# Another order for SyncE's placement of the value pieces of batch 0: nine, nine and seven behind the turns and loads of three passes, in place of rows of 8 and 17

## What is computed

```python
x = x + xattn(layernorm(x), ctx_768, Wq, bq, Wk, bk, Wv, bv, Wo, bo)
x = x + ffn(layernorm(x), expert_embeddings, first_linear, second_linear)

# xattn: 16 heads of width 32
attn = softmax(clip(einsum('bhqd,bhkd->bhqk', q, k) * scale))
x = einsum('bhqk,bhkd->bqhd', attn, v).reshape(B, Nq, Cq) @ Wo + bo
```

## Time and profile before

| | us |
|---|---|
| median of three runs | 1437.44 |
| lowest and highest of them | 1436.42, 1442.03 |
| the profiled execution, its own time | 1439.36 |
| its span on the core | 1437.6 |
| TensorE busy | 1320.3 (92%) |
| VectorE busy | 952.7 (66%) |
| ScalarE busy | 805.5 (56%) |
| GpSimd busy | 739.0 (51%) |

### The profile page before, as it was taken

How to read it: one execution, slowest core, us unless ns; L and a number is a source line. 1 busy time by engine, 2 the same in 40 slices (tenths; PEclk the granted TensorE clock), 3 DMA queues, 4 the chain that set the end, 5 groups by cost and what they waited for, 6 DMA issues and landing times.

```text
span 1437.6 us, 30587 instructions
## 1 busy us (share of the span) xinstructions
PE 1320.3 (92%) x12330; PEld 780.1 (54%) x12330; DVE 952.7 (66%) x1808; ACT 805.5 (56%) x1272; POOL 739.0 (51%) x781
## 2 busy tenths in 40 slices
PE   7649999989998999997849999999999999999996
PEld 3436777767676777774527444444444444444442
DVE  8768898979889787888775545454454545455421
ACT  4658888868998899987354514233241514334210
POOL 3458878877888778887323332242514224251301
PEclk9959999989999899999969999999999999999998
DMA  6157998968887786888433564565646555654401
GB/s 197 54 117 179 221 237 210 236 175 184 210 222 167 180 175 181 184 221 210 125 115 103 164 183 141 154 177 138 157 125 180 144 151 166 156 140 125 103 16 43
DMA packets 319574, 228.88 MB, mean 159 GB/s; under 512 B 253305, under 2 KB 253689, under 8 KB 319434
## 3 DMA queue, kind: packets, MB, share of 16 engines
q1 hardware_dynamic: 304074, 176.28, 49.4%
q0 software_dynamic: 15360, 50.66, 12.1%
HBM read 118.98 MB, written 50.86 MB: 118 GB/s over the span
## 4 chain that ended last, share of the span: by engine, by line
PE 74%; DVE 10%; POOL 8%; issue 3%; ACT 2%; SPq 1%; DMA 1%; DVEq 0%; POOLq 0%; ACTq 0%
PE ps L1210 23%; PE ps L1196 23%; PE ps L1096 9%; PE ps L1026 7%; PE ps L1077 3%; PE ps L1113 2%; POOL sd L547 2%; PE ps L1010 2%; DVE sm L1461 1%; PE ps L1049 1%; POOL qT L527 1%; DVE x L1483 1%; POOL ph L553 1%; PE ps L999 1%; POOL oT L533 1%
## 5 line engine op out<-in xcount | busy, mean ns | idle before, releaser
L1196 PE MATMUL ps<-xT,w1s 128*128 128x512 f16 (+1 forms) x1632 | 336.3, 368 | 1.9 <-DVE xT L1726 1.5
L1210 PE MATMUL ps<-w2s,hT 128*128 128x512 f16 x1536 | 332.8, 379 | 0.0
L848 ACT ACTIVATE hT<-ps 128x512 f16<-128x512 f32 (+1 forms) x136 | 77.5, 572 | 356.3 <-PE ps L1196 292.5
L1196 PEld LDWEIGHTS ps<-xT,w1s 128*128 128x128 f16 x1632 | 160.7, 99 | 175.3 <-issue 1.9
L1210 PEld LDWEIGHTS ps<-w2s,hT 128*128 128x128 f16 x1536 | 150.3, 98 | 181.2
L598 POOL DMA_INDIRECT out_dram<-ys,idx x64 | 71.8, 1121 | 278.0 <-DVE ys L1766 278.0
L1026 PE MATMUL ps<-xnT,wqh 128*128 128x256 f16 x1536 | 198.3, 281 | 8.2 <-ACT partq L736 8.1
L1096 PE MATMUL ps<-woh,oT 128*128 128x512 f16 x768 | 182.2, 386 | 5.4 <-POOL oT L533 5.2
L1756 DVE SCALAR_TENSOR_TENSOR hT<-ps,hT 128x512 f16<-128x512 f32 (+1 forms) x136 | 88.4, 658 | 140.4 <-ACT hT L848 88.7
L1766 DVE SCALAR_TENSOR_TENSOR ys<-ps,gs,og 128x512 f32<-128x512 f32 x64 | 48.1, 751 | 189.4 <-PE ps L1210 189.4
L553 POOL TENSOR_TENSOR ph<-sd,ph 128x1232 f16<-128x1232 f32 x64 | 162.2, 2535 | 18.7 <-ACT ph L759 18.0
(11 more groups left out here) (206 smaller groups left out, 2013.0 us busy)
## 6 DMA issues: line engine op xcount, KB each, us to landing
xr<-x SPq DMA_DIRECT2D x64, 256.0 KB, 3.4
xrow_dram<-x SPq DMA_DIRECT2D x64, 256.0 KB, 3.6
out_dram<-x SPq DMA_DIRECT2D x64, 256.0 KB, 4.0
stage<-w1T SPq DMA_DIRECT2D x8, 2048.0 KB
stage<-w2T SPq DMA_DIRECT2D x8, 2048.0 KB, 8.4
xt<-x SPq DMA_DIRECT2D x59, 256.0 KB, 3.2
xs<-x SPq DMA_DIRECT2D x56, 256.0 KB, 4.1
wqf<-wq SPq DMA_DIRECT2D x1, 1024.0 KB, 7.2
```

What stands on the lines that cost most here:

```text
L1196: ins = pe.matmul(hb[z][:, 0:wide], w1s[e % 2][:, a, k, ic * P:(ic + 1) * P], xT[:, 4 * b + k, cols], start=(k == 0 and i == 0), stop=(k = ...
L1210: ins = pe.matmul(yb[z][:, :], hT[:, a, k, s * P:(s + 1) * P], w2s[e % 2][:, b, k, :], start=(k == 0 and i == 0), stop=(k == 7 and i == 2))
```

## The change

SyncE's loop places batch 0's 25 pieces at the end of the loads of three passes. In pass -5 nine pieces follow the loads of tiles 9, 13 and 14. In pass -4 nine follow the transpose of tile 0 and the loads of tiles 10 and 15. In pass -3 the last seven follow the transpose of tile 1 and the loads of tiles 11, 16 and 17. (values_place returns at once for a number beyond the last piece.) Nothing else differs, on any engine.

```diff
             for h in range(-7, T):
-                if h == -5:
-                    for k in range(8):
-                        values_place(0, k)
                 p_T(h + 4)
-                if h == -4:
-                    for k in range(8, len(pieces)):
-                        values_place(0, k)
                 if h + 14 >= RT + XT:
                     load_x(h + 14)
                 if h >= 1:
                     load_r(h + 4)
                 for t in stats_at(h + 1):
                     load_s(t)
+                if -5 <= h <= -3:
+                    for k in range(9 * (h + 5), 9 * (h + 6)):
+                        values_place(0, k)
                 if h == -2:
                     sp.wait_ge(S["made"], 5)
                     sp.wait_ge(S["bor"], 1)
```

## The result

The changed kernel takes 1433.42 us, the median of 13 runs (1431.66 to 1435.01), against 1437.44 in 13 runs of the kernel before (1436.30 to 1442.03). The ratio is 0.9965, with a 95% interval of 0.9955 to 0.9975: faster by 0.35%. The 13 runs of each tell this from no change, though it is less than the 0.5% that the prediction had named as the bound. The forecast was 1434.5.

The account below looks back on a forecast made before the run. It took SyncE's issuing to bound the stretch from 66 to 125 us; -11.6 (stall gone) + 8.7 (given back) = -2.9 us from the median of 1437.44 gave 1434.5 us, range 1430.5 to 1439.5.

Parts of the forecast that it names:

- The stall: VectorE's 11.6 us wait for tile 15 of x goes: the tile lands at 82.2, against a request at 82.36.
- SyncE's queue: SyncE's new order of pieces, transposes and loads, followed with old durations; last piece issued from 97.3 to 98.15 us.
- What is late next: TensorE's first product with the values waits for the last piece, landing 2.2 us from issue: 99.5 us, 2.8 later.
- P: Start of TensorE's first product with the values, forecast at 99.5 us against 96.73 before.
- From P to the end of the stretch: Work from P to tile 0's output projection: GpSimd's subtraction at P + 9.1, 108.6 against 111.5, so 2.9 us earlier.
- the 8.7 given back: What the first product's new wait returns on the path, set against the 11.6 us stall: net -2.9 us.
- rival (a): TensorE's clock returns sooner behind P: P + 7.9 instead of P + 9.1, gain 4.1, 1433.3 us; chance 0.13.
- The rule of the Trainium skill: TensorE: sustained activity releases the clock throttle, idle brings it back; dense work behind P would earn 1.3 us.
- (b): The last seven pieces land late; at 9.3 us landing, P is 106.6 and the kernel loses 4.2: 1441.6 us; chance 0.13.
- (c): SyncE or GpSimd, 3 us from their own limit, give the gain back before 118.48: 1437.4 us; chance 0.13.
- (d): Pieces issue faster than 0.85 us and don't hold the first product; VectorE's 96.3 bounds, gain 8.8, 1428.6 us; chance 0.06.
- the price of the new order: SyncE's slack from 60.28 to 66.49 us, which held 8 pieces, is now spent in waiting.

Follow-up runs that it names:

- e4: The kernel before with 28 extra, unused TensorE products in front of the first product with the values; 1438.12 us, ratio to before 1.0006.
- e6: The kernel before with 44 extra, unused TensorE products in front of the first product with the values; ratio to before 0.9984, on another chip.
- e9: The changed kernel measured once more, nothing altered; 1433.13 us, ratio to the kernel before 0.996.
- e3: The changed kernel with 36 extra, unused TensorE products in front of the first product with the values; 1433.22 us, ratio to before 0.9963.
- e8: The changed kernel with eight pieces before pass -5, then 4, 6 and 7 behind the loads of passes -5, -4, -3; ratio to before 0.991, repeated 0.9936.

## Why the prediction came out right, and where it was off

**The stall.** Right. VectorE was to ask for tile 15 at 82.36 and find it landed; it took it at 82.60 with no gap.

**SyncE's queue.** Right within 0.5 us at every step as the times stand: nine pieces at 67.0 (67.28), the transposes at 74.6 and 86.6 (75.10 and 87.04), seven pieces from 92.2 to 98.15 (91.83 to 97.67). The trace as a whole runs 0.32 us late, and with this taken off the last seven come 0.7 to 0.8 us early. One term was too long: the second transpose took 3.16 us of issue, the lower bound of the text, and not 4.03. The 4.03 belonged to its old place. Where the second transpose is issued right behind a load into xs, it takes 4.03 to 4.26 us (the kernel before, e4, e6); where pieces stand between, 3.07 to 3.58 (all others). Why is not shown.

**What is late next.** Right. The wait moved from the transpose to the pieces. From the issue of the last one to the product it took 2.26 us (2.02 of it to landing), where 2.2 was taken from the bias copies. P came at 99.05, which is 98.7 on the old trace's time, against the predicted 99.5; the transpose's shorter issue is most of what made it early.

**From P to the end of the stretch.** GpSimd's subtraction was put at P + 9.1. It came at 107.62, P + 8.6. The difference of 0.5 us is the clock: the projection took 2.19, not 2.74. The granted clock was 0.62 from 101.9 to 104 and 1.00 in the 2 us behind:

```profile
101.90:104.00 2.10, 2.10 (x24) 1.52 (x13) 1.74 (x2) 0.49 (x2) 1.15 (x1) 0.62 0.89 245
104.00:106.00 2.00, 1.42 (x14) 1.12 (x13) 2.00 (x2) 1.78 (x3) 0.84 (x2) 1.00 0.45 157
```

(Windows, columns as in the earlier trace rows.) So the forecast of 2.9 us was small by two terms, 0.8 us of P and 0.5 of clock: 4.2, which the stretch shows. In the text's sum, the 8.7 given back was no term of its own but what this walk left of the 11.6; measured, it is 7.4. The text took 0 for the clock, out of bounds of 0 and 1.3 us; it was 0.5 in this trace. In the second trace of the same kernel (e9) the subtraction comes at P + 8.0, which is rival (a)'s P + 7.9 almost in full. So rival (a) was true in part, more or less of it from one execution to the next. That its 1433.3 is so near the measured 1433.42 is in part luck, since it had P 0.8 us too late. The rule of the Trainium skill (TensorE: Matmul & The Clock Gate, Part 1) was borne out: dense work behind P brought the clock back earlier (1.00 granted from 104 us, 5 us behind P, where before it was 0.50 up to 108.6, 12 us behind P). The part on idle time, that a longer gap brings it back down, shows in e3: full to the end of the fill, 0.50 after 5.3 us of idle time.

**The other rivals.** (b) fell: the pieces land in 2 us, even behind three loads and a transpose. (c) fell: SyncE's backlog ended at 106.4, and the fourth transpose was not ready before 110.17. (d) fell: the pieces' issues were no faster (7.62 and 7.78 us for nine, 5.84 for seven), and the pieces held the product. Its next bound was VectorE, at 96.3. Where P does come earlier than that, in e8, it is GpSimd that sets the end. Tile 0's output projection came at 114.62, or 114.3 on the old trace's time, where 115.6 was forecast.

**What the prediction did not see.** It called the waste of the slack "the price of the new order" and put 2.8 us on P, but it summed the change as a whole and did not ask which part earns and which costs. The runs show that the 17 pieces behind the loads earn all of it, and that the rest of the change, three groups with the first eight out of the slack, only costs.

## What to carry to other kernels

When one queue issues both loads that other engines wait for and a row of small transfers that are needed later, put the loads ahead of the row, and leave in front of them only what fits the time in which the queue waits anyway. Before splitting a row, find for each group whether it stands in slack or on the path: here 17 pieces moved behind two loads took 7 us off the stretch, and eight moved out of the slack gave 3 of them back. Once a wait goes, read what the engines behind it do (here GpSimd without a gap) before paying for more.

## What the runs showed that I had not expected

With VectorE no longer idle, its low half of the output weights runs beside GpSimd's bias rows, and one of GpSimd's small casts, 0.60 us in the kernel before, takes 2.68. GpSimd in the kernel before, then GpSimd and VectorE in the changed kernel:

```profile
85.08 0.60 POOL L562 CAST bot<-bos 1x512 bf16<-1x512 f32 x1
```

```profile
83.52 0.60 POOL L559 CAST bot<-bos 1x512 bf16<-1x512 f32 x1
84.20 1.16 POOL L565 TENSOR_TENSOR bos<-bos,bot 1x512 f32<-1x512 f32 x1
85.42 2.68 POOL L559 CAST bot<-bos 1x512 bf16<-1x512 f32 x1
```

```profile
83.60 0.55 DVE L1335 TENSOR_SCALAR nw<-mv 128x4 f32<-128x4 f32 x1
...
84.39 1.00 DVE L1341 TENSOR_SCALAR mv<-mv 128x4 int32<-128x4 int32 x1
85.30 2.34 DVE L1856 SCALAR_TENSOR_TENSOR woh<-wof,scr,woh 128x2048 f16<-128x2048 f32 x1
```

The cast starts 0.12 us after VectorE's instruction and ends 0.46 after its end, and it took 2.68 or 2.69 in every version in which VectorE no longer waits there. The Trainium skill (SBUF — State Buffer, SBUF: two separate sides) says that a VectorE instruction with two SBUF inputs and a GpSimd instruction that reads SBUF exclude each other for the whole instruction; the rows agree. That it is this lock was not tried by itself. VectorE is held up too: two of its small instructions ahead of that one, 0.17 us each in the kernel before, take 0.55 and 1.00 here, and each ends within 0.03 us of the end of the GpSimd instruction beside it. In the changed kernel the 2.1 us are hidden, since GpSimd waits for ScalarE later. In e8's order, where GpSimd has no gap from this cast to the end of the stretch, they may be a part of the bound; moving the bias rows was not tried.
